# A two-layer graph attention kernel: scores of a pair in one step, hops spread over two turns, a loop of two turns

## What is computed

```python
# layer A, 8 heads of 32
q, k, v = x @ Wq.T + bq, x @ Wk.T + bk, x @ Wv.T + bv
pros = softmax(where(adj == 0, -16384, q_h @ k_h^T))
z = v
for _ in range(4):                       # four hops
    z = 0.9 * (pros @ z) + 0.1 * v
x1 = layernorm(x + z) * gamma + beta
# layer B, on x1
nx = layernorm(x1) * ln1_g + ln1_b
q, k, v = nx @ wq + bq, nx @ wk + bk, nx @ wv + bv
attn = softmax(q_h @ k_h^T / sqrt(32) + where(adj > 0, 0.1 * adj * adj, -inf))
x2 = x1 + (attn @ v) @ wo + bo
out = x2 + gelu(layernorm(x2) @ w1 + b1) @ w2 + b2      # 256 -> 1024 -> 256
```

## Time and profile before

| | us |
|---|---|
| median of 3 runs (lowest, highest) | 2408.23 (2403.92, 2408.38) |
| the profiled execution | 2406.89 |
| its span, first to last instruction | 2405.3 |

### The profile page before, as it was taken

One profiled execution on the slowest core, in us unless ns is written; L12 is line 12 of the kernel. 1 busy time (PEld: TensorE's weight loads), 2 busy tenths in 40 slices (PEclk: granted clock), 3 DMA queues, 4 the chain that ended last, 5 costly groups with the idle time before them and its releaser, 6 DMA issues.

```text
span 2405.3 us, 81001 instructions
## 1 busy us (share of the span) xinstructions
PE 2318.2 (96%) x29492; PEld 2165.6 (90%) x29492; DVE 1738.8 (72%) x7457; ACT 1917.6 (80%) x6462; POOL 1571.8 (65%) x1610
## 2 busy tenths in 40 slices
PE   2789999999999999999999999999999999999997
PEld 2689999999999999999999999999999999999987
DVE  2577777777777777777777777777777777777774
ACT  0578888888888888888888888888888888888884
POOL 0566766666666666666766666676676666666662
PEclk9899999999999999999999999999999999999999
DMA  3010110110110010011011011011011011011000
GB/s 98 15 32 21 35 33 20 35 33 21 34 33 24 30 33 30 24 33 35 20 33 35 20 33 35 20 33 35 20 35 33 20 35 33 22 32 33 25 22 14
DMA packets 95390, 72.27 MB, mean 30 GB/s; under 512 B 9600, under 2 KB 95104, under 8 KB 95360
## 3 DMA queue, kind: packets, MB, share of 16 engines
q1 hardware_dynamic: 95360, 71.87, 9.9%
HBM read 55.06 MB, written 16.78 MB: 30 GB/s over the span
## 4 chain that ended last, share of the span: by engine, by line
PE 92%; ACT 3%; DVE 2%; issue 1%; POOL 1%; DMA 0%; ACTq 0%; SPq 0%; DVEq 0%; POOLq 0%
PE ring_ps L328 42%; PE ring_ps L444 14%; PE ring_ps L390 13%; PE ring_ps L382 10%; PE ring_ps L410 5%; PE score_ps L373 5%; PE ring_ps L338 2%; ACT zT L493 2%; ACT probs L480 0%; DVE stats L642 0%; DVE probs L587 0%; POOL rstd L745 0%; DVE w_low L545 0%; POOL x L752 0%; POOL x L754 0%
## 5 line engine op out<-in xcount | busy, mean ns | idle before, releaser
L480 ACT ACTIVATE probs<-probs,negmax 128x128 f32<-128x128 f32 x2048 | 793.2, 391 | 71.4 <-DVE negmax L587 70.7
L736 POOL TENSOR_TENSOR probs<-probs,rinv 128x512 f32<-128x512 f32 x512 | 556.5, 1108 | 270.7 <-DVE rinv L601 270.7
L480 ACT ACTIVATION_READ_ACCUMULATOR probs<-probs,negmax 128x1 f32 x2048 | 389.2, 190 | 0.0
L587 DVE CUSTOM_DVE_ANT_0 probs<-score_ps,mask_B 128x128 f32<-128x128 f32 x1024 | 230.3, 286 | 126.2 <-issue 126.2
L328 PE MATMUL ring_ps<-inT_C_high,w_high 128*128 128x256 f32 x1024 | 308.9, 302 | 1.7 <-DVE inT_C_low L568 1.7
L328 PE MATMUL ring_ps<-inT_C_high,w_low 128*128 128x256 f32 x1024 | 287.3, 281 | 0.0
L328 PE MATMUL ring_ps<-inT_C_low,w_high 128*128 128x256 f32 x1024 | 287.2, 280 | 0.0
L382 PE MATMUL ring_ps<-ident,probs 128*128 128x128 f32 x2048 | 283.4, 277 | 3.4 <-ACT hT_high L507 1.5
L444 PE MATMUL ring_ps<-w_high,hT_high 128*128 128x256 f32 x1024 | 284.1, 277 | 0.3 <-DVE hT_low L660 0.3
L444 PE MATMUL ring_ps<-w_high,hT_low 128*128 128x256 f32 x1024 | 283.6, 277 | 0.0
L444 PE MATMUL ring_ps<-w_low,hT_high 128*128 128x256 f32 x1024 | 283.5, 277 | 0.0
(11 more groups left out here) (149 smaller groups left out, 7350.4 us busy)
## 6 DMA issues: line engine op xcount, KB each, us to landing
xT_sb<-in_xT_dram SPq DMA_DIRECT2D x64, 256.0 KB, 2.8
x_sb<-in_x_dram SPq DMA_DIRECT2D x64, 256.0 KB, 3.3
out_dram<-x SPq DMA_DIRECT2D x128, 128.0 KB, 1.7
adj_A<-in_adj_dram SPq DMA_DIRECT2D x64, 128.0 KB, 2.6
adj_B<-in_adj_dram SPq DMA_DIRECT2D x64, 128.0 KB, 2.1
probsT_A<-in_L_gnn_w_dram SPq DMA_DIRECT2D x1, 1024.0 KB, 7.9
probsT_B<-in_L_gnn_w_dram SPq DMA_DIRECT2D x1, 1024.0 KB, 10.0
probs<-in_L_gnn_Wq_dram SPq DMA_DIRECT2D x1, 256.0 KB, 2.7
```

Source lines behind the costliest of these rows:

```text
L480: e = act.activation(probs[:, u, h, :], probs[:, u, h, :], ACT.Exp, bias=negmax[:, u, h:h + 1], scale=-1.0, accum_out=sums[:, u, h:h + 1])
L587: t = dve.tensor_tensor_reduce(probs[:, u, h, :], score_ps[:, r, half * P:(half + 1) * P], mask[l][:, b, :], -1.0, HIGHEST, ALU.add, ALU.m ...
L736: pool.tensor_tensor(probs[:, u, hs, :], probs[:, u, hs, :], rinv[:, u, hs].unsqueeze(2).to_broadcast([P, HR, P]), ALU.mult).then_inc(s_pr ...
```

## The change

Four things are changed together.
- The scores of both graphs of a pair are one step, `sA` or `sB`, of 32 matmuls. It uses all columns of the four banks and waits for all maxima of the other layer's pair; the first maxima step alone waits for it.
- The lags go up to 5. `z0`, `z1`, `z2` and their turnings back have lag 2 like `z3`, `h3` has lag 3; layer A's maxima and exponentials have lag 1, its probabilities lag 1, layer B's scores lag 3 and the rest of B lags 4 and 5. `v_A`, `xv` and `probsT_A` become two buffers each, used in turn by pair (`side`), `z` three, `zT` four.
- The loop body holds two turns, so that the buffer's side is a constant. Turns 0 to 5 are written out, then 29 passes of two turns, then five turns.
- All steps stand in a new order.

```diff
 ORDER = """
+tC/5 eB10/4 xs/1 vB/4 z0/2 h3/3 eB11/4 y0/3 u0/5 rB1/4 wA0/2 h0/2 lx/2 u1/5 lt/0 eb/3 wA1/2 u2/5 msA/1 b1/4 c0/5 n0/3
+c1/5 sA/1 i2/5 b2/5 z1/2 pB00/4 u3/5 mA00/1 laA/1 xv/2 pB10/4 mA01/1 c2/5 pB01/4 c3/5 vA/1 eA00/1 y1/3 h1/2 pB11/4
+n1/3 d0/5 eA01/1 wB0/4 z2/2 mA10/1 rA0/1 pv/4 laB/2 tB/3 mA11/1 d1/5 i0/3 eA10/1 eA11/1 h2/2 qB/3 rA1/1 wB1/4 kB/3
+pA00/1 o/4 mB00/3 y2/4 sB/3 mB01/3 g/3 z3/2 eB00/3 i1/3 pA01/1 kA/0 pA10/1 st/5 n2/4 pA11/1 msB/3 mB10/3 mB11/3 eB01/3
+qA/0 rB0/3
 """
...
+    def side(self, name):
+
+        return (self.odd + LAG[name]) % 2
...
-        v = {l: sb(f"v_{l}", [P, GB, H]) for l in "AB"}
-        xv = sb("xv", [P, GB, H])
-        z = sb("z", [P, GB, H])
+        v_A = [sb(f"v_A{i}", [P, GB, H]) for i in range(2)]
+        v_B = sb("v_B", [P, GB, H])
+        xv = [sb(f"xv{i}", [P, GB, H]) for i in range(2)]
+        z = [sb(f"z{k}", [P, GB, H]) for k in range(HOPS - 1)]
...
-        probsT = {l: sb(f"probsT_{l}", [P, GB, NH, P]) for l in "AB"}
-        zT = sb("zT", [P, GB, C, P])
+        probsT_A = [sb(f"probsT_A{i}", [P, GB, NH, P]) for i in range(2)]
+        probsT_B = sb("probsT_B", [P, GB, NH, P])
+        zT = [sb(f"zT{k}", [P, GB, C, P]) for k in range(HOPS)]
...
         def run(eng, steps):
-            for i in range(DEPTH + 1):
+            head = DEPTH + 1 + (G - DEPTH - 1) % 2
+            for i in range(head):
                 steps(Body(i, G))
-            with eng.Fori(DEPTH + 1, G) as i:
-                steps(Body(i))
+            with eng.Fori(head, G - 1, 2) as i:
+                steps(Body(i, odd=head % 2))
+                steps(Body(i + 1, odd=(head + 1) % 2))
             for i in range(G, G + DEPTH):
                 steps(Body(i, G))
...
-                def scores(name, l, b):
+                def scores(name, l):
                     emptied(name, "q" + l)
                     emptied(name, "k" + l)
                     old, back = body.before(SCORE_ORDER, name, 1)
                     if old:
-                        pe.wait_ge(s_masked[f"m{old[1:]}1"], body.count(old, back))
-                    for h in range(NH):
-                        r, c = h % HR, h // HR
-                        mm = pe.matmul(score_ps[:, r, c * P:(c + 1) * P],
-                                       qT[l][r * HD:(r + 1) * HD, c, b * P:(b + 1) * P],
-                                       kT[l][r * HD:(r + 1) * HD, c, b * P:(b + 1) * P], start=True, stop=True)
+                        pe.wait_ge(s_masked[f"m{old[1:]}{GB - 1}1"], body.count(old, back))
+                    for b in range(GB):
+                        for h in range(NH):
+                            r, c = h % HR, h // HR
+                            mm = pe.matmul(score_ps[:, r, (b * C + c) * P:(b * C + c + 1) * P],
+                                           qT[l][r * HD:(r + 1) * HD, c, b * P:(b + 1) * P],
+                                           kT[l][r * HD:(r + 1) * HD, c, b * P:(b + 1) * P], start=True, stop=True)
                     mm.then_inc(s_full[name], 1)
...
                 def maxima(name, l, b, half):
                     u = UNIT[l, b]
-                    if half == 0:
-                        dve.wait_ge(s_full[f"s{l}{b}"], body.count(name))
+                    if b == 0 and half == 0:
+                        dve.wait_ge(s_full["s" + l], body.count(name))
                         dve.wait_ge(s_mask[l], body.count(name))
                         wait_apart()
...
                 def shares(name):
-                    if body.second(name):
-                        pool.wait_ge(s_out["h3"], body.count(name, 1))
+                    sum_ = xv[body.side(name)]
+                    if body.later(name, 2):
+                        pool.wait_ge(s_out["h3"], body.count(name, 2))
```

More of the change, by code:

```diff
@@ L56 @@
     KINDS[f"v{_l}"] = ("values", _l)
+    KINDS[f"s{_l}"] = ("scores", _l)
     KINDS[f"la{_l}"] = ("load_adj", _l)
@@ L88, with __init__ @@
 class Body:
-    def __init__(self, i, pairs=None):
+    def __init__(self, i, pairs=None, odd=None):
         self.i, self.pairs = i, pairs
+        self.odd = i % 2 if odd is None else odd
         self.names = [n for n in NAMES if self.runs(n)]
@@ L106, in count, with later @@
         return self.counts[n]
-    def second(self, name):
-        return self.pairs is None or self.pair(name) > 0
+    def later(self, name, n=1):
+        return self.pairs is None or self.pair(name) >= n
+    def side(self, name):
+        return (self.odd + LAG[name]) % 2
     def before(self, order, name, apart):
@@ L268, in load_turned @@
                 def load_turned(name):
-                    if body.second(name):
+                    if body.later(name):
                         sp.wait_ge(s_split, body.count(name, 1))
@@ L401, in hop @@
                                 emptied(name, f"pA{b}{half}")
-                    mix(name, z if k else v["A"], probsT["A"])
+                    mix(name, z[k - 1] if k else v_A[body.side(name)], probsT_A[body.side(name)])
                 def turn_back(name, k):
@@ L417, in attend @@
                             emptied(name, f"pB{b}{half}")
-                    mix(name, v["B"], probsT["B"])
+                    mix(name, v_B, probsT_B)
                 def output(name):
@@ L487, in turn_probs @@
                         full(name)
-                        act.activation(probsT[l][:, b, 0:HR, :], ring(name).rearrange("p (h n) -> p h n", h=HR),
+                        dst = probsT_A[body.side(name)] if l == "A" else probsT_B
+                        act.activation(dst[:, b, 0:HR, :], ring(name).rearrange("p (h n) -> p h n", h=HR),
                                        ACT.Copy).then_inc(s_out[name], 1)
@@ L571, in values @@
                 def values(name, l):
-                    if l == "A" and body.second(name):
+                    if l == "A" and body.later(name):
                         dve.wait_ge(s_xv, body.count(name, 1))
@@ L575, in values @@
                     row = bvA_row if l == "A" else bvB_row
-                    dve.tensor_tensor(v[l][:, :, :], ring(name).rearrange("p (b n) -> p b n", b=GB),
+                    dst = v_A[body.side(name)] if l == "A" else v_B
+                    dve.tensor_tensor(dst[:, :, :], ring(name).rearrange("p (b n) -> p b n", b=GB),
                                       row[:, :].unsqueeze(1).to_broadcast([P, GB, H]), ALU.add).then_inc(s_out[name], 1)
@@ L605, in turn_probs @@
                         full(name)
-                        dve.tensor_copy(probsT[l][:, b, HR:NH, :], ring(name).rearrange("p (h n) -> p h n", h=HR))\
+                        dst = probsT_A[body.side(name)] if l == "A" else probsT_B
+                        dve.tensor_copy(dst[:, b, HR:NH, :], ring(name).rearrange("p (h n) -> p h n", h=HR))\
                            .then_inc(s_out[name], 1)
@@ L612, in turn_back @@
                     if k < HOPS - 1:
-                        dve.scalar_tensor_tensor(out=z[:, :, :], in0=v["A"][:, :, :], scalar=ALPHA / KEEP ** (k + 1), in1=ps,
+                        dve.scalar_tensor_tensor(out=z[k][:, :, :], in0=v_A[body.side(name)][:, :, :], scalar=ALPHA / KEEP ** (k + 1), in1=ps,
                                                  op0=ALU.mult, op1=ALU.add).then_inc(s_out[name], 1)
                     else:
-                        if body.second(name):
+                        if body.later(name):
                             dve.wait_ge(s_x1, body.count(name, 1))
                         dve.wait_ge(s_xv, body.count(name))
-                        dve.scalar_tensor_tensor(out=y[:, :, :], in0=ps, scalar=KEEP ** HOPS, in1=xv[:, :, :],
+                        dve.scalar_tensor_tensor(out=y[:, :, :], in0=ps, scalar=KEEP ** HOPS, in1=xv[body.side(name)][:, :, :],
                                                  op0=ALU.mult, op1=ALU.add).then_inc(s_out[name], 1)
```

20 lines of the change are left out of this document (9 added, 11 removed).

## The result

The changed kernel takes 2431.43 us (median of 4 runs, 2428.21 to 2433.01), the kernel before 2408.31: a ratio of 1.0098, interval 1.0081 to 1.0116. It is slower by 1%, where I had forecast 2361 us and a range of 2335 to 2414. The profiled execution has a span of 2426.4 us, 21 more than the profiled one before.

What follows compares the result with a forecast made beforehand. TensorE was taken to bound the kernel; 55.0 us start, 64 turns of 34.90 and 70 us edges gave 2358.6, with 1.6 outside and 1.3 to the median 2361 us, range 2335 to 2414.

Steps and rivals of the forecast that it cites:

- What bounds the kernel: Full turns: TensorE works 2143.25 of 2146.90 us, so only fewer or cheaper TensorE steps or its few waits save time.
- Sum of a turn: One full turn on TensorE: 35.785 - 0.42 - 0.34 - 0.13 = 34.90 us, bounds 34.5 to 35.3.
- merged scores: TensorE's score steps: four of 16 at 0.66 us become two of 32 at 1.10, taken as -0.42 us per turn.
- z2 beside pv: Two mixes now adjacent on TensorE: between 0 and -0.12 us per turn, taken as -0.09.
- transposes behind a mix: TensorE transposes after a mix take 0.42 us instead of 0.36; such places rise from one to four, +0.17 per turn.
- The wait of h0: TensorE after z0 waits for ScalarE's copy; 0.12 to 0.13 us exposed per turn goes, as h3 and u0 stand between.
- either of their two rates: TensorE projections run 0.113 or 0.117 to 0.118 us apart, cause unknown; all 180 matmuls of a turn differ by 0.8 us.
- The cover of the waits: Full turns: other TensorE work hides the remaining waits, booked at 0; closest margin 0.1 to 0.2 us, at qA behind pA01.
- rival 2: New waits replace the one removed in full turns: 0.5 us per turn comes back, 2393 us; chance 0.13.
- Edges: Filling and emptying, ten partial turns instead of six: 60.1 us plus 10 taken, 70; bounds +0 to +40.
- Loop of two turns: The loop's jumps back, halved in number: each costs at most some hundredths of a us, booked at 0.
- rival 1: Doubled loop body leaves TensorE's instruction memory: 28 jumps stall 2.0 us each, +56, 2417 us (2389 to 2453); chance 0.24.

Runs made afterwards that it cites:

- the straight version: The changed kernel with all 69 turns written out and no loop: 2350.48 us, ratio 0.9739 to the kernel before.
- experiment 5: The changed kernel with all turns written out, each pair's scores split again into two steps of 16: 2442.14 us.
- experiments 1 and 4: All turns written out without a loop: the changed kernel 2350.48 us, ratio 0.9739; the kernel before 2414.15 us, ratio 1.0005.
- experiment 2: The kernel before in its own order, with two turns per loop pass instead of one: 2554.36 us, ratio 1.0580.
- experiment 6: The changed kernel with only the loop's jump moved from behind qA to behind pv: 2465.49 us, ratio 1.0254 to the kernel before.

## Why the prediction was wrong, point by point

- **What bounds the kernel**: right. Sixty-four turns of TensorE's stream and the edges are the time; in the versions with a loop that isn't held the jumps come on top.
- **Sum of a turn**: 34.90 forecast, 34.88 measured. Term by term: merged scores -0.42, in the trace 4 x 0.66 less 2 x 1.10 = -0.44; z2 beside pv, taken at -0.09, is 1.88 to 1.89 for 64 against 2 x 1.01, -0.13; a merged score group 1.10, forecast 1.10; transposes behind a mix 0.41, forecast 0.42. The wait of h0 is gone: the chain of the straight version has no ScalarE piece between 999.93 and 1036 where the earlier trace rows have one each turn. That projections would go on at either of their two rates was left open and is still open; the sum came out in the middle.
- **The cover of the waits**: right, and as thin as stated. No new wait appears in the full turns, so rival 2 fell; experiment 5 shows that 1.34 us of delay in the maxima bring one of 1.06 us.
- **Edges**: 70 us forecast; the straight version has 2348.7 - 54.6 - 64 x 34.88 = 61.8, the kernel before 60.1. Ten partial turns idle no more in all than six: the term was 8 us too high, in the end that I had called "+0".
- **Loop of two turns: this is the step that failed.** That a jump costs at most some hundredths, booked at 0, was read from the kernel before, where the body is held, and carried over to a body of twice the size. The runs showed 2.31 us for each of 28 jumps and 1.55 more after eight of them, 77 us in all. The mechanism was seen, as rival 1, and the trace of before could not tell the capacity. But I gave it 0.24, though by the capacity that it quotes the body of 1,920 instructions stays only if it lies well and no block ahead displaces the first. With the fetch ahead taken as the likely case, my own price made 2417 us.
- **Within rival 1** the price was low. The stall was put at 2.0 us and costs 2.31 (28 jumps, +9 us), and the falls of the clock (8 x 1.55 = +12 us) were not in it at all, though the profile of before shows the lower clock in all of its thin stretches. With both: 2361 - 8 (edges) + 65 + 12 = 2430; measured 2431.
- **The range** reached to the middle of rival 1 only, and so missed the time by 17 us.

So the gain was there, 58 us by the straight version (62 against the kernel before as run beside it), and 81 us were given back at the jumps.

## What to carry to other kernels

Before a loop body is made longer, count the instructions of the busiest engine in it: here 1438 on TensorE were held and 1678 were not, and a jump in a body that isn't held cost 3.7 to 4.2 us less what that engine had queued, plus what a fallen clock costs; in the one body that began some 100 instructions before the end of a block a second wait of 1.9 us followed each time. In the profile the sign is the number of packets in the instruction queue while the loop runs, and a wait on "issue" that comes as often as the jumps, or twice as often. Where two turns must differ, try all turns written out: straight code was fetched here at no cost that shows.

## What the runs showed of the hardware

- Falls of the clock from a stop of 2 to 4 us: TensorE was full before and after, and the granted clock went to 1.2 GHz for 3.4 us (or 6.8) after 8 of 28, 12 of 13, 19 of 27 jumps in the changed orders, and 21 of 29 in the order of before. Not one fall lies in the full turns of the two straight versions of experiments 1 and 4. In experiment 2 it adds up to 46 us to the 95 of the waits; a single fall of 6.8 us about doubles the price of its jump.
- The place of the jump alone moved the time by 34 us (experiment 6), with the same instructions in the same order in the loop.
- Projections run at 113 or at 118 ns per matmul for whole steps in every version. In the kernel before one and the same step does either in different turns; I found no cause.
